# The residual's reload in a four-layer GNN and FFN kernel: issued by SyncE in the experts' block instead of at the beginning of the next block

## What is computed

```
x = x + gnn0(layernorm(x))     # sum over the edges, then four dense layers with batch norms
x = x + ffn0(layernorm(x))     # mixture of 8 experts, each node goes to its best two
x = x + gnn1(layernorm(x))     # graph attention with 4 heads
x = x + ffn1(layernorm(x))     # the better half of the nodes goes through one wide FFN
```

```
h = layernorm(x)
y = h @ W;  el = y @ Wl.T;  er = y @ Wr.T
e = exp(leaky_relu(el[src] + er[dst]));  w = e / segment_sum(e, src)[src]
out[:, head] = elu(segment_sum(w[:, head] * y[dst], src) + b)
```

## Time and profile before

| what | us |
|---|---|
| median of 3 runs (2200.25 to 2207.63) | 2200.62 |
| the profiled execution's own time | 2197.58 |
| its span, first to last instruction | 2195.9 |
| PE busy | 1830.5 |
| DVE busy | 1374.3 |
| POOL busy | 1347.9 |
| ACT busy | 670.3 |

### The profile page before, as it was taken

The page is one execution under the profiler, slowest core; times in us unless marked ns, Lnnn a source line. Parts: engine busy times, 40 slices in busy tenths (PEclk is TensorE's granted clock), DMA queues, the critical chain, the costliest instruction groups (busy, mean ns, idle before and its releaser), DMA issues. The chain is left out here.

```text
span 2195.9 us, 36674 instructions
## 1 busy us (share of the span) xinstructions
PE 1830.5 (83%) x9636; PEld 1305.5 (59%) x9637; DVE 1374.3 (63%) x3193; ACT 670.3 (31%) x1334; POOL 1347.9 (61%) x1358
## 2 busy tenths in 40 slices
PE   2898999888899799663899999947878887885888
PEld 2776777666344345562666666645656665664666
DVE  7766654444755686778733333346777777777766
ACT  4000000000455665635633333332111111111874
POOL 3777777776277777742566666527777777774000
PEclk8555555555999799855999999977898889887999
DMA  8333333333000300272122222252111111113002
GB/s 247 98 105 103 105 105 105 105 104 90 0 1 1 60 1 1 83 282 88 30 39 39 39 39 39 30 123 40 28 28 28 28 29 28 29 28 13 1 1 59
DMA packets 95358, 132.05 MB, mean 60 GB/s; under 512 B 34959, under 2 KB 66334, under 8 KB 95293
## 3 DMA queue, kind: packets, MB, share of 16 engines
q0 software_dynamic: 57312, 87.64, 18.3%
q1 hardware_dynamic: 37981, 43.65, 6.9%
HBM read 109.24 MB, written 21.96 MB: 60 GB/s over the span
## 5 line engine op out<-in xcount | busy, mean ns | idle before, releaser
L590 POOL DMA_INDIRECT rec_d<-rec,posd x392 | 396.0, 1010 | 166.9 <-issue 125.6
L491 PE MATMUL psA<-oh,G 128*128 128x128 f32 x1568 | 444.2, 448 | 61.2 <-DMA G<-xn_d,gat_i 29.8
L1670 POOL DMA_INDIRECT g<-tab_d,recs x416 | 395.1, 950 | 160.3 <-issue 126.5
L306 POOL DMA_INDIRECT G<-xn_d,gat_i x392 | 376.6, 961 | 146.1 <-issue 137.4
L491 PEld LDWEIGHTS psA<-oh,G 128*128 128x128 f32 x1568 | 351.6, 313 | 153.7 <-issue 98.2
L1819 PE MATMUL psS<-vv,oh 128*125 128x260 f32 x832 | 288.7, 494 | 90.8 <-DVE acc L1751 90.8
L835 PE MATMUL psZ<-z,W 128*128 (+1 forms) x1344 | 264.4, 360 | 24.0 <-DVE z L734 24.0
L1819 PEld LDWEIGHTS psS<-vv,oh 128*125 128x125 f32 x832 | 160.9, 225 | 188.8 <-DVE acc L1751 161.3
L441 DVE TENSOR_TENSOR accT<-accT,psA 128x256 f32 x392 | 164.9, 421 | 166.4 <-PE psA L491 140.5
L636 ACT ACTIVATE z<-psZ,vec 128x500 f32 (+2 forms) x112 | 70.7, 633 | 638.1 <-PE psZ L828 527.9
L835 PEld LDWEIGHTS psZ<-z,W 128*128 128x128 f16 x1344 | 124.7, 99 | 163.7 <-issue 37.0
(11 more groups left out here) (323 smaller groups left out, 2433.3 us busy)
## 6 DMA issues: line engine op xcount, KB each, us to landing
raw<-in_L_ffn_w SPq DMA_DIRECT2D x16, 682.0 KB, 8.6
g<-tab_d,recs POOLq DMA_INDIRECT x416, 2.5
G<-xn_d,gat_i POOLq DMA_INDIRECT x392, 2.7
rec_d<-rec,posd POOLq DMA_INDIRECT x392
raw<-in_L_ffn_w SPq DMA_DIRECT2D x16, 384.0 KB, 10.1
wst<-in_L_gnn_W SPq DMA_DIRECT2D x9, 512.0 KB, 6.8
x<-in_x SPq DMA_DIRECT2D x5, 560.0 KB
xn_d<-x SPq DMA_DIRECT2D x5, 560.0 KB
```

The costliest lines, as they stand in the source:

```text
L306: pool.indirect_dma_start(out=G[:, i, :], out_offset=None, in_=xn_d, in_offset=bass.IndirectOffsetOnAxis(ap=gat_i[:, t:t + 1], axis=0)).th ...
L491: last = nc.tensor.matmul(psA[i // 2][:, i % 2, h, :], G[:, i, 128 * h:128 * (h + 1)], oh[:, i, :], start=True, stop=True)
L590: pool.indirect_dma_start(out=rec_d.rearrange("p (t r) -> (p t) r", r=2), out_offset=bass.IndirectOffsetOnAxis(ap=posd[:, t:t + 1], axis=0 ...
L1670: pool.indirect_dma_start(out=g3[:, n % BODY, j, :], out_offset=None, in_=tab_d, in_offset=bass.IndirectOffsetOnAxis(ap=recs[:, t, 1:2], a ...
```

## The change

SP gets two waits and ten issues at the end of its list in the experts' block: it waits until all scatters of `yv` have landed and then issues the loads of all five chunks of the residual there. They count on the semaphores `s_raw[0]` (chunk 0) and `s_raw[1]` (chunks 1 to 4), which live on from the experts' weights and stand at 64. In the next block the ten loads are gone from SP's list, `s_x4` is gone, and DVE waits on `s_raw`: for chunk 0 as before for its two loads, for each of chunks 1 to 4 until all four have landed (64 + 128).

```diff
@@ the experts' block, SP
                 for e in range(X):
                     if e not in EARLY:
                         load_expert(sp, e)
+                for i in range(2):
+                    sp.wait_ge(s_yst[i], 16 * (T2 // 2))
+                for c in range(5):
+                    cs = slice(5 * c, 5 * c + 5)
+                    for lo, hi in SPLIT:
+                        sp.dma_start(x2[lo:hi, cs, :],
+                                     x2_d[0:N, :].rearrange("(b p) d -> p b d", p=PB)[lo:hi, cs, :]).then_inc(s_raw[min(c, 1)], 16)
@@ the next block, SP
-                residual(0)
                 sp.dma_start(wt[:, :], a["L1_gnn_WT"]).then_inc(s_wt, 16)
                 for j, name in enumerate(("r", "l")):
                     sp.dma_start(wlr[:, j, :], a["L1_gnn_W" + name]).then_inc(s_wlr, 16)
                 sp.dma_start(wx[:, :, NH:NH + OD], a["L1_gnn_W"].rearrange("(k p) n -> p k n", p=128)).then_inc(s_wlr, 16)
-                for c in range(1, 5):
-                    residual(c)
                 sp.wait_ge(s_one, 1)
@@ the next block, DVE
                 for c in range(5):
-                    dve.wait_ge(s_x4[c], 32)
+                    dve.wait_ge(s_raw[min(c, 1)], 64 + (128 if c else 32))
                     normalise(dve, ch, x2, xn3, c, s_v4, s_d4, s_n4)
```

More of the change, by code:

```diff
@@ L1468, in program @@
         tab_d = dram("tab_d", (N, RW))
-        s_x4 = [sem(f"s_x4{c}") for c in range(5)]
         s_wt = sem("s_wt")
```

## The result

| what | before | after |
|---|---|---|
| time, median of six runs each, us | 2202.28 | 2210.27 |
| lowest to highest, us | 2200.19 to 2207.63 | 2207.07 to 2213.62 |
| the profiled execution, us | 2197.58 | 2213.62 |
| its span, us | 2195.9 | 2211.9 |

The ratio is 1.0039, with a 95% interval of 1.0025 to 1.0052: the change makes the kernel **slower by 8.0 us** by the medians, 5.5 to 11.5 by the interval.

The account below looks back on a forecast made before the run. It took the wait for the small weights as the bound, ending 1.1 us last, the residual second. Step 3's +6.3 us, the only term added, on the median 2200.62 gave 2206.9 us; range 2199.7 to 2210.6.

Parts of the forecast that it names:

- Step 1: End of SP's experts' block: the first residual issue comes at 1434.0, 4.4 us earlier than 1438.42.
- Step 2: Barrier between blocks: ten issues make SP late by 1.5 to 3.6 us, hidden beneath the weights' wait, so not added.
- Step 3: SP's load queue: small weights queue behind the whole residual, so `wx` lands 6.3 us later (5.5 to 7.0).
- Step 4: Next block: 2.7 us from `wx` to root, then 29.0 unchanged; chunk 0's 4.63 lost in DVE's some 8 for ACT.
- Step 5: DVE's coarser wait for chunks 1 to 4 costs nothing, as all the residual lands before `wx`.
- The faster transfer: Rival: the residual moves at 308 GB/s at the boundary, `wx` lands 3.9 us later, 2204.5 us; chance 0.11.
- the weights that overtake: Rival: weights do not queue behind the residual, the late barrier binds, +0.6 to +2.7 us, 2202.3 us; chance 0.10.
- Not slower: Rival: weights first and ten issues fit beneath POOL's drain; block starts as before, gain 0.9 us, 2199.7 us; chance 0.04.
- The cold TensorE: Rival: PE's clock stays low to the block's end, +7.1 us on top of 6.3, 2214.0 us; chance 0.05.

Follow-up runs that it names:

- w_behind: The kernel before, with the four small weight loads issued behind all ten residual loads in the next block; 2213.84 us against 2203.09, ratio 1.0055.
- all_early_mended: The change with small weights ahead of the residual, `acc` memset behind DVE's last instruction, a semaphore per chunk; 2202.49 us against 2202.06, ratio 1.0000.
- chunk0_early: The change with only chunk 0 issued in the experts' block, chunks 1 to 4 behind the weights in the next, common semaphore kept; 2210.29 us, ratio 1.0029.
- w_ahead_late_memset: w_ahead with POOL's memset of `acc` moved behind DVE's last instruction of the block; 2205.92 us against 2203.60 before, ratio 1.0018.
- w_ahead: The change with the four small weight loads also in the experts' block, ahead of the residual; 2207.78 us against 2203.09 before, ratio 1.0018.
- root_first: The change with ACT's wait for the weights' products and its two copies behind its first square root; 2205.96 us against 2203.09 before, ratio 1.0009.
- two_chunks: The change with weights issued before the scatter waits, only chunks 0 and 1 early, a semaphore per chunk; 2200.74 us against 2203.60 before, ratio 0.9987.
- chunk0_fine: chunk0_early with a semaphore count of its own for each chunk; 2202.23 us against 2203.60 before, ratio 0.9998.

## Why the prediction was right in its mechanism and wrong in its answer

*Step 1, ten issues earlier*: right. They begin at the landing (1439.07 against 1439.0).

*Step 2, SP late at the barrier, by 1.5 to 3.6 us, but beneath the weights' wait*: right. It was 3.5, and in the changed kernel it is hidden. w_behind shows that the loss needs no late barrier, and all_early_mended that the late barrier is the next thing to bind.

*Step 3, the weights behind the whole residual*: right as a mechanism, and the term was undersized: +6.3 taken, 5.5 to 7.0 as its bounds, 7.0 in the trace. The rate wasn't at fault. From 1441 to 1454 the core of the changed kernel moved 252 GB/s (the columns of the earlier trace rows), above the 238 that was taken:

```profile
1441.00:1454.00 13.00, 0.00 (x0) 0.00 (x0) 5.46 (x12) 0.00 (x0) 5.57 (x2) 0.50 1.12 252
```

What was missing is at the end of the queue: `wx` landed 2.1 us behind that stretch. The trace's packets show how. The 256 packets of `wx` (256 bytes each) moved within 0.5 us before, from 1442.44 on; with the change they take 3.1 us, from 1452.04 to 1455.14. Behind the first of them at least 256 of the residual's packets still come, and half of the packets of `recs`, which SP issued later, go ahead of the last. So at its end the queue does not go strictly in turn, and a small load waits for its last packet. Why the packets spread so is not shown.

*Step 4, from there as before*: right, 2.7 and 29.0 us. The wait gained at chunk 0 was lost in the wait for ACT, of 6.43 us, with 3.1 more hidden in the held-up step on 5 columns: 9.5 together, for "some 8". That hold-up by the memset was in none of the terms. In the kernel before it could not be seen, the memset being over at 1444.0, before that step ran at 1445.43.

*Step 5, the coarser wait costs nothing*: right for this change, under the condition it named, that the weights come last; chunk0_early shows 7.39 us without that, with chunks 1 to 4 issued in the next block, and w_ahead_late_memset 3.39 us with all of them early.

**The step that failed** is the last sentence of the sum: "About 0.5%, or 11 us, is what a measurement of this kernel can tell from no change, so this counts as no change." No row of the prediction stands behind the 0.5%. Six runs of each kernel told the ratio to within 0.14% either way, and by that +6.3 us, 0.29%, is a slower kernel; measured were +8.0 us, 0.39%. Three single runs that lay 7 us apart made the bound look right, but the error of a median is smaller than the spread of single runs. The chance of no change, 0.93, therefore stood on a mechanism that I held to be a loss. In the sum itself the step that was off is the term of step 3, 7.0 for 6.3. The time, 2210.27, is at the upper edge of the range, in part by luck: the forecast's own 2206.1 to 2207.6 was left, and what holds it is the 3.0 us added at the top for another reason. Of the 3.4 us above 2206.9, 1.7 are the median of the kernel before, 2200.62 in three runs and 2202.28 in six, 0.7 the term of step 3, and 1.0 is not seen in the trace and lies within the interval.

*The rivals.* The faster transfer (+3.9) and the weights that overtake (+0.6 to +2.7) are out: `wx` landed at 17.1, and the core moved 252 GB/s with PE and ACT idle, not the 308 of the rival. (That was a mean over 2 us and not chunk 0's best; from 1440.5 to 1441 it moved 375.) "Not slower" needed the ten issues to fit beneath the drain; they took 7.46 us, not 4.2. The cold TensorE would have shown in the 29.0 us behind the root, which are unchanged.

## What to carry to other kernels

Before moving a large transfer earlier, find which load ends the wait, and ask what small load it now pushes back in the same queue: here 3.2 MB ahead of 130 KB cost 7 us, and the order small first, then as much of the large one as fits beneath the barrier's drain, gained 4, both in the trace. Issuing early has its own price when it makes the issuer late at a barrier: here the barrier opened 3.5 us later with ten issues, and 5.5 us later with the weights' four ahead of them. When one wait goes, look at every condition that it covered, a common semaphore or a memset on a neighbouring engine: each showed only after the one in front had been removed.

## What the hardware showed that I had not expected

**A DVE step held by a POOL memset.** The `TENSOR_SCALAR` on 125x5 elements took 3.27 us in the changed kernel, in w_ahead and in root_first, and 1.58 us in two_chunks, instead of 0.17. In chunk0_early it took 2.85 us, in chunk0_fine 3.12. In all six it ended within 0.1 us of the end of the memset of `acc`, while the batch norm statistics beside the same memset kept their 1.73 us. The Trainium skill, SBUF — State Buffer, section Who interferes with whom, says that DVE and GpSimd share one pair of ports under an exclusive lock, that `tensor_scalar` is among the operations that can ask for it, in a mode that uses both ports, and that whoever comes second is blocked for the whole of the other's instruction. The trace agrees with the blocking, and w_ahead_late_memset shows it by taking the memset away (0.17 us); the ports and the mode themselves are in no trace here.
